# Two-layer block: the finished result kept in phase order along the length axis

## The reference, cut to what matters

```
x: [32, 128, 2048] float32
x = x + L0_ffn(L0_cond(x))       # layer 0: two products along channels and length
c = conv1d(x, 9 taps, 4 groups) + context     # layer 1, [32, 128, 2048]
t = c.reshape(4096, 2048)[:, perm]            # permutation of the length axis
t = gelu(t @ up[h]) @ down[h]    # 16 heads of 128 positions, hidden 512
t = t[:, argsort(perm)]          # permuted back
out = x + t
```

## Time and profile before

| | us |
|---|---|
| median of 3 runs | 2666.65 (2665.01 to 2669.32) |
| the profiled execution's own time | 2668.66 |
| its span, first to last instruction | 2666.7 |
| PE busy | 2576.5 (97%) |
| DVE busy | 1835.0 (69%) |
| ACT busy | 1003.1 (38%) |
| POOL busy | 957.7 (36%) |
| DMA packets, bytes | 419587, 541.04 MB |

### The profile page before, as it was taken

How to read it: one execution, slowest core, us unless ns; L and a number is a source line. 1 busy time by engine, 2 the same in 40 slices (tenths; PEclk the granted TensorE clock), 3 DMA queues, 4 the chain that set the end, 5 groups by cost and what they waited for, 6 DMA issues and landing times. The chain is left out here.

```text
span 2666.7 us, 39124 instructions
## 1 busy us (share of the span) xinstructions
PE 2576.5 (97%) x12090; PEld 2112.6 (79%) x12090; DVE 1835.0 (69%) x2671; ACT 1003.1 (38%) x1631; POOL 957.7 (36%) x835
## 2 busy tenths in 40 slices
PE   8899999999999999999999999999999999999885
PEld 6678888888888788887888778888888888888674
DVE  6555555865555755475444768888888888888675
ACT  3211112311122322232222555555555555555562
POOL 2275645456554454233223212222222222222221
PEclk9999999999999999999999999999999999999997
DMA  9855644765545667475545744667767777677667
GB/s 307 303 182 181 203 162 150 253 196 199 187 161 182 224 219 221 155 252 192 164 155 182 222 143 131 181 218 219 216 215 220 219 218 219 217 217 218 191 195 229
DMA packets 419587, 541.04 MB, mean 203 GB/s; under 512 B 36440, under 2 KB 273840, under 8 KB 419376
## 3 DMA queue, kind: packets, MB, share of 16 engines
q1 hardware_dynamic: 317168, 305.04, 38.3%
q10 hardware_dynamic: 77376, 154.27, 15.4%
q0 software_dynamic: 24832, 79.16, 9.2%
HBM read 309.72 MB, written 228.61 MB: 202 GB/s over the span
## 5 line engine op out<-in xcount | busy, mean ns | idle before, releaser
L427 PE MATMUL ps_c<-w_hi,ring_hi 128*128 128x512 f32 x1792 | 714.3, 399 | 12.7 <-DVE r_early L931 6.7
L427 PE MATMUL ps_c<-w_hi,ring_lo 128*128 128x512 f32 x1792 | 708.5, 395 | 0.0
L427 PE MATMUL ps_c<-w_lo,ring_hi 128*128 128x512 f32 x1792 | 708.3, 395 | 0.0
L574 ACT ACTIVATE ring_hi<-raw_n 128x512 fp32r<-128x512 f32 x384 | 240.7, 631 | 896.2 <-DVE raw_n L871 243.9
L1295 POOL DMA_INDIRECT y_d<-y_s,idx x128 | 147.5, 1152 | 750.5 <-ACT y_s L1465 644.3
L427 PEld LDWEIGHTS ps_c<-w_hi,ring_hi 128*128 128x128 f32 x1792 | 338.4, 189 | 92.2 <-DVE ring_lo L910 13.4
L1432 ACT ACTIVATE kern<-ps_up 128x512 f32<-128x512 f32 x512 | 306.5, 599 | 261.2 <-PE ps_up L1318 242.6
L427 PEld LDWEIGHTS ps_c<-w_hi,ring_lo 128*128 128x128 f32 x1792 | 338.0, 189 | 79.8
L427 PEld LDWEIGHTS ps_c<-w_lo,ring_hi 128*128 128x128 f32 x1792 | 338.4, 189 | 76.7
L1550 DVE TENSOR_TENSOR g_lo<-kern,g_hi 128x512 fp32r<-128x512 f32 x512 | 354.7, 693 | 48.5 <-ACT g_hi L1436 32.1
L931 DVE TENSOR_TENSOR r_early<-ps_c,r_early 128x512 f32<-128x512 f32 x256 | 176.8, 690 | 286.3 <-PE ps_c L427 286.2
(11 more groups left out here) (199 smaller groups left out, 3852.8 us busy)
## 6 DMA issues: line engine op xcount, KB each, us to landing
u_d<-raw_n ACTq DMA_DIRECT2D x64, 512.0 KB, 3.2
x_d<-r_early ACTq DMA_DIRECT2D x128, 256.0 KB, 3.4
x_d<-x_s ACTq DMA_DIRECT2D x128, 256.0 KB, 2.7
raw_n<-u_d SPq DMA_DIRECT2D x64, 512.0 KB, 3.5
u_s<-x_d SPq DMA_DIRECT2D x496, 64.0 KB, 2.7
z_d<-x_s SPq DMA_DIRECT2D x120, 256.0 KB
rear<-y_d SPq DMA_DIRECT2D x120, 256.0 KB, 6.2
rear<-x_d SPq DMA_DIRECT2D x112, 256.0 KB
```

What stands on the lines that cost most here:

```text
L427: mm = nc.tensor.matmul(bank, a[:, dc, :], w[k][:, dc, :], start=(first and dc == 0 and n == 0), stop=(dc == 3 and n == 2), skip_group_che ...
L574: nc.scalar.activation(ring_hi[g % RING][:].rearrange("p a n -> p (a n)"), ring_raw[p][k], ACT.Copy).then_inc(hi_ready, 1)
```

## The change

A final unit now covers one phase s = c (512 positions l = 4q + c) in place of 512 neighbouring positions. The y rows of a phase are every fourth row of `y_d`, 8 KB apart; the pieces stay 512 B and there are still 512 of them. x1 of a phase is one run of 2 KB per channel. The add reads x1 and writes the sum contiguously. The result is stored in phase order, in a DRAM tensor `[NB, C, S, Q]`, and the host permutes the finished array.

```diff
-        x1_s = [rear[:, 2 + j, :].rearrange("p (s q) -> p s q", s=S) for j in range(2)]
+        x1_s = [rear[:, 2 + j, :] for j in range(2)]
...
+        def phase_rows(y, c):
+            return y.rearrange("(l p s) r -> s p l r", p=P, s=S)[c]
... load_final (SP)
-                sp.dma_start(yt_s[j], y_d[1 - parity][c * 512:(c + 1) * 512, h // 4 * C:(h // 4 + 1) * C]
-                             .rearrange("(l p) r -> p l r", p=P)).then_inc(yt_in[j], 16)
+                sp.dma_start(yt_s[j], phase_rows(y_d[1 - parity], c)[:, :, h // 4 * C:(h // 4 + 1) * C]).then_inc(yt_in[j], 16)
...
-                sp.dma_start(x1_s[j], x1_d[b, :, :, c * P:(c + 1) * P]).then_inc(x1_in[j], 16)
+                sp.dma_start(x1_s[j], x1_d[b, :, c, :]).then_inc(x1_in[j], 16)
... load_last_x1 (SP) and the POOL loads of last_x1: the same edit; finish (SP): phase_rows in the same way
... store_out (SP) and the tail's stores (ACT)
-                sp.dma_start(out[b, :, c * 512:(c + 1) * 512], o_s[j]).then_inc(o_out[j], 16)
+                sp.dma_start(out[b, :, c, :], o_s[j]).then_inc(o_out[j], 16)
... take_final (DVE); the tail's add is edited in the same way
-                nc.vector.tensor_tensor(o_s[j].rearrange("p (q s) -> p q s", s=S),
-                                        ps_f[:, 0, :].rearrange("p (q s) -> p q s", s=S),
-                                        x1_s[j].rearrange("p s q -> p q s"), ALU.add).then_inc(o_ready, 1)
+                nc.vector.tensor_tensor(o_s[j], ps_f[:, 0, :], x1_s[j], ALU.add).then_inc(o_ready, 1)
... host
-    out = nc.dram_tensor("out_0_dram", (NB, C, L), F32, kind="ExternalOutput").ap()
+    out = nc.dram_tensor("out_0_dram", (NB, C, S, Q), F32, kind="ExternalOutput").ap()
-    return r.results[0]["out_0_dram"]
+    return r.results[0]["out_0_dram"].swapaxes(-1, -2).reshape(NB, C, L)
```

More of the change, by code:

```diff
@@ L1069, in layer1_block @@
         last_x1 = (last_x1 + last_x1)[:H]
-        last_x1 = [room.rearrange("p (s q) -> p s q", s=S) for room in last_x1]
         last_yt = yt_s + [t.rearrange("p (l r) -> p l r", l=4) for t in t_s]
-        last_sum = o_s + [x1.rearrange("p s q -> p (s q)") for x1 in x1_s]
+        last_sum = o_s + x1_s
         last_ps = [ps_f[:, 0, :], ps_c[:, 0, :]]
+        def phase_rows(y, c):
+            return y.rearrange("(l p s) r -> s p l r", p=P, s=S)[c]
         def last_unit(v):
@@ L1187, in load_last_x1 @@
                     sp.wait_ge(zt_done, STEPS)
-                sp.dma_start(last_x1[v], x1_d[b, :, :, c * P:(c + 1) * P]).then_inc(last_x1_in[v], 16)
+                sp.dma_start(last_x1[v], x1_d[b, :, c, :]).then_inc(last_x1_in[v], 16)
             def finish():
@@ L1199, in finish @@
                     wait(sp, last_fin, v - 3)
-                    sp.dma_start(last_yt[v % 4], y_d[(BLOCKS - 1) % 2][c * 512:(c + 1) * 512, v // 4 * C:(v // 4 + 1) * C]
-                                 .rearrange("(l p) r -> p l r", p=P)).then_inc(last_yt_in[v % 4], 16)
+                    sp.dma_start(last_yt[v % 4], phase_rows(y_d[(BLOCKS - 1) % 2], c)[:, :, v // 4 * C:(v // 4 + 1) * C]
+                                 ).then_inc(last_yt_in[v % 4], 16)
             def store_out(k, h):
@@ L1304, in _ @@
                 wait(pool, last_o, v - ROOMS + 1)
-                pool.dma_start(last_x1[v], x1_d[b, :, :, c * P:(c + 1) * P]).then_inc(last_x1_in[v], 16)
+                pool.dma_start(last_x1[v], x1_d[b, :, c, :]).then_inc(last_x1_in[v], 16)
             pool.wait_ge(y_out[0], 16 * (STEPS // 2))
@@ L1472, in _ @@
                 act.wait_ge(last_o, v + 1)
-                act.dma_start(out[b, :, c * 512:(c + 1) * 512], last_sum[v % 4]).then_inc(last_o_out[v % 4], 16)
+                act.dma_start(out[b, :, c, :], last_sum[v % 4]).then_inc(last_o_out[v % 4], 16)
             for j in range(4):
@@ L1581, in _ @@
                 wait(dve, last_o_out[v % 4], 16 * (v // 4))
-                nc.vector.tensor_tensor(last_sum[v % 4].rearrange("p (q s) -> p q s", s=S),
-                                        last_ps[v % 2].rearrange("p (q s) -> p q s", s=S),
-                                        last_x1[v].rearrange("p s q -> p q s"), ALU.add).then_inc(last_o, 1)
+                nc.vector.tensor_tensor(last_sum[v % 4], last_ps[v % 2], last_x1[v], ALU.add).then_inc(last_o, 1)
 def build(nc, x, cond_t, fside, w0, b0, w1, b1, w2, b2, cond_w, bias_k, w_t, bias, lora_a, lora_b, coeffs, scales,
```

## The result

The changed kernel took 2682.11 us (median of 5 runs, 2680.73 to 2683.99) against 2666.65 before; the ratio of the two is 1.0058, 95% interval 1.0043 to 1.0072. The forecast was 2663.7 with a range up to 2672. The profiled execution took 2681.51 us, with a span of 2679.7.

What follows compares the result with a forecast made beforehand. PE was taken to bound the steady loop, chains of waits the last block and tail. Tail adds -1.0, last-block add -1.0 and tail x1 fetches -1.0 gave -3.0 us: 2663.7 for the median, range 2656 to 2672.

Steps and rivals of the forecast that it cites:

- the last block's: Last block, where a ring of waits through gathers, ACT and POOL's scatter sets the time: add -1.0 us, gathers 0.
- The gather's term: Last block, twelve gathers on the chain beside x1 fetches: between -8.9 and +7.0 us, taken as 0.
- The add's term: Last block, quicker add in front of DVE's splits on the chain: at most 1.9 us gained, taken as -1.0 us.
- The third rival: Last block, gather loses its turn to larger x1 packets: +7.0 there, +5.0 in all, 2671.7 us; chance 0.09.
- Its "against": Last block: shortest chain gather, 3.31 us, was under the lone one though x1 fetches go out beside them.
- The steady loop: Loop bound by PE without idle: DVE's 44 us less busy time there was held to be worth nothing.
- The new add: DVE's add of x1, now contiguous: 0.690 us in place of 1.085.
- SP's issue: SP's issue of an x1 fetch: from 0.577 us to about 0.328, worth nothing.
- The packets: All 128 x1 fetches in 2 KB packets: 49,152 packets fewer, 419587 to about 370,400, bytes unchanged.
- The tail: After the last block: -1.0 us from three adds on the chain and -1.0 us from quicker x1 fetches.
- The y pitch: y fetches with rows 8 KB apart in place of 2 KB: 0 to +0.78 us per unit, taken as 0.
- first y fetches at block boundaries: Steady loop: 15 such fetches, each us beyond 7.27 would cost about 15 us.

Runs made afterwards that it cites:

- e7_before_hold_store: Kernel before, with the store of the result held in the last 19 steps until DVE's first g_lo behind the add; 2664.12 us, ratio 0.9993.
- e8_fetch_hold_store: Kernel before, with the store held in the last 19 steps and x1 fetched by phase in 2 KB packets; 2670.04 us, ratio 1.0019.
- e4_fetch_and_add: Kernel before, with x1 fetched by phase and the add made contiguous, y by neighbouring rows; 2680.27 us, ratio 1.0060.
- e1_y_only: Kernel before, with only the y fetches by phase (rows 8 KB apart); 2664.1 us, ratio 1.0002.
- e5_hold_x1: Changed kernel, with the x1 fetch and the store behind it held in the last 19 steps until DVE's first g_lo; 2661.11 us, ratio 0.9987.
- e3_add_only: Kernel before, with only the add made contiguous, x1 still fetched in 512 B runs; 2672.69 us, ratio 1.0033.
- e10_no_x1: Changed kernel without the x1 fetches of the last 19 steps and the add's wait for them; 2670.53 us, ratio 1.0018.

## Why the prediction was wrong

**The step that failed** is the last block's, in two terms. "Whether the gather gains or loses is open ... I take 0", with +7.0 as the upper end, and "-1.0 us" for the add in the last block. Together they forecast -1.0 us; the 19 steps became 16.0 us longer.

- The gather's term was put at 0 because its ends had opposite signs, not because a row spoke for 0. The fetch alone measured +0.34% (about 9 us) and made the 19 steps 6.4 us longer in its profile, near the upper end of +7.0. What the term left out is that the gather is also met sooner.
- The add's term had the wrong sign. I looked at what waits behind the add on DVE, which is little, and not at what its end releases: `o_ready` frees the x1 buffer, and SP's fetch was released by it in these steps. The path DVE's add, SP's x1 fetch, POOL's gather is missing from the prediction. In the waits of SP that I had read, this one was listed (L1178 for DVE's L1529, 54.6 us in 19 times), and I did not use it. The add alone measured +0.33% (about 9 us) and made the 19 steps 8.1 us longer in its profile.
- The third rival was right that larger x1 packets cost the gather time (about 6 us between `e7_before_hold_store` and `e8_fetch_hold_store`). That this goes by turns is not shown. Its "against", a shortest gather of 3.31 us, was a gather at the block boundary with no fetch beside it, SP standing in its wait for the last scatter. That one was no evidence, and the gathers of 3.4 us that did have a fetch beside them had one in 512 B packets.

**The rest, by its steps.** The steady loop: no gain and no loss, as forecast. The new add 0.683 us for a forecast 0.690. SP's issue in these steps 0.33 us, as forecast. The packets fell by 45,698 to 373,889, not by 49,152: 119 fetches by SP show the change (119 x 384 = 45,696), the nine by POOL do not in that count. The tail: -2.0 forecast, -2.2 measured (and 37.9 us from the first y fetch's issue to the end, where 37.5 was forecast). That was luck. The path is another: the 6.61 us wait for a store is gone, one y fetch takes 11.16, and one add lies on the chain in place of three. And the forecast had put the gain down to the add and the x1 fetches, with 0 for y. The profiles say otherwise: with both parts and neighbouring y rows (`e4_fetch_and_add`) the tail takes 42.4 us, and with the y fetch by phase alone (`e1_y_only`) 41.0. All six profiles with y by phase have 40.2 to 41.4 us, all eight without 42.0 to 45.8.

The y pitch: 0 forecast, ratio 1.0002 measured for the whole kernel. The Trainium skill, DMA: Bandwidth & Descriptors, section "Latency and other measured facts", has the full rate at a pitch of 512 KiB, less at 2 MiB and half at 4 MiB; the prediction stretched it to pieces 1 MB apart, which the page does not list. At 8 KB and 1 MB these runs show no loss. The rule of the same page of the Trainium skill on turns between queues ("Queues, rings and completion order") pointed toward the loss; what the runs show is that size and start both count, and turns themselves show in no trace here. One count in the prediction was wrong without effect: with 8 blocks there are 7 first y fetches at block boundaries, not 15.

Shown: both the start of SP's transfers against the gather and the form of the x1 fetch set the gather's time, and each makes about half of this change's loss (+0.33% and +0.34%). Holding the transfers takes away both halves. Shown by the packet records: in the changed kernel x1's packets are served before the gather's. Open: why the early fetch in 512 B packets slows a gather that is served first, and whether the second half comes from the packet size or the pace of the issue.

## What to carry to other kernels

Before an instruction is made faster, read what its end releases, and not only what waits behind it: here a quicker add let a bulk transfer start 0.4 us sooner, too close behind the one transfer that the critical ring waits for. Where a ring of small steps waits for a gather, hold bulk transfers of other queues until the gather is under way; one wait on a semaphore that already exists took the changed kernel from 1.0058 to 0.9987 of the kernel before, about 19 us. And price a transfer on the critical chain together with everything issued within a microsecond of it.

## What the runs showed of the hardware

A gather of 256 KB issued by POOL took 3.2 to 3.8 us when SP's 256 KB fetch in 2 KB packets followed 1.6 us later (`e5_hold_x1`), and 4.7 to 5.4 us when it followed 0.5 us later (the changed kernel), where the fetch's packets were served first. In 512 B packets at +0.5 us it took 4.3 to 5.0 us (`e3_add_only`). A store has the same kind of effect as a fetch (4.30 us at +0.54, `e10_no_x1`). Reading 512 B rows at an 8 KB pitch in place of 2 KB did not change the kernel's time (ratio 1.0002). DVE's add of 512 columns took 0.68 us with x1 contiguous and 1.09 us with its elements 512 B apart. The issue of a fetch of 128 runs of 2 KB holds SP for 0.33 us, that of 512 runs of 512 B into the same rows for 0.55.
